# Cross attention over eight batches: in the first batch, who normalises, who makes the low parts, and where the transposes are written

## The reference

```python
q = einsum('bcn,dc->bnd', x, Wq) + bq
k = einsum('bcn,dc->bdn', ctx, Wk) + bk[:, None]
v = einsum('bcn,dc->bdn', ctx, Wv) + bv[:, None]
attn = softmax(einsum('bnd,bdm->bnm', q, k), axis=2)
out = einsum('bcm,bnm->bcn', v, attn) + x
```

## Time and profile before

| | |
|---|---|
| median of 3 executions | 667.35 us (667.12 to 668.11) |
| the profiled execution's own time | 666.91 us |
| its span | 664.7 us |
| TensorE matmul busy | 650.7 us, 98% |
| VectorE, ScalarE, POOL busy | 461.1, 285.0, 138.2 us |
| granted TensorE clock over the span | 0.996 |

### The profile page before, as it was taken

How to read it: one execution, slowest core, us unless ns; L and a number is a source line. 1 busy time by engine, 2 the same in 40 slices (tenths; PEclk the granted TensorE clock), 3 DMA queues, 4 the chain that set the end, 5 groups by cost and what they waited for, 6 DMA issues and landing times.

```text
span 664.7 us, 8316 instructions
## 1 busy us (share of the span) xinstructions
PE 650.7 (98%) x2852; PEld 533.5 (80%) x2852; DVE 461.1 (69%) x506; ACT 285.0 (43%) x372; POOL 138.2 (21%) x57
## 2 busy tenths in 40 slices
PE   8978899999999999999999999999999999999998
PEld 5766788888888888888888888888888888888886
DVE  5956768696586785786767867769668696586541
ACT  6656523456235362354433743337432456135120
POOL 0266300053002430033200430006300063002100
PEclk9999899999999999999999999999999999999999
DMA  8900732874428733496325863167621875325352
GB/s 314 329 6 1 175 96 78 223 239 125 126 77 233 232 96 121 114 308 160 101 88 139 306 167 101 64 158 269 172 95 63 200 265 135 121 71 139 72 158 88
DMA packets 94253, 100.09 MB, mean 151 GB/s; under 512 B 7328, under 2 KB 69024, under 8 KB 94240
## 3 DMA queue, kind: packets, MB, share of 16 engines
q1 hardware_dynamic: 94240, 99.91, 50.5%
HBM read 51.64 MB, written 16.78 MB: 103 GB/s over the span
## 4 chain that ended last, share of the span: by engine, by line
PE 90%; DVE 3%; POOL 1%; DMA 1%; issue 1%; ACT 1%; SPq 1%; DVEq 0%; POOLq 0%
PE acc_ps L854 51%; PE acc_ps L823 23%; PE s_ps L793 8%; PE s_ps L801 4%; PE s_ps L802 4%; DMA stage<-in_x_dram 1%; DVE pt_lo L532 1%; POOL blocks L299 1%; DVE negmax L592 1%; POOL probs L299 1%; DVE k_ll L532 0%; PE acc_ps L924 0%; ACT pt_hi L326 0%; SPq L256 0%; DVE vt_lo L532 0%
## 5 line engine op out<-in xcount | busy, mean ns | idle before, releaser
L854 PE MATMUL acc_ps<-pt_hi,vt_hi 128*128 128x512 f32 x512 | 199.4, 390 | 0.6 <-issue 0.6
L854 PE MATMUL acc_ps<-pt_hi,vt_lo 128*128 128x512 f32 x512 | 199.3, 389 | 0.0
L854 PE MATMUL acc_ps<-pt_lo,vt_hi 128*128 128x512 f32 x512 | 199.3, 389 | 0.0
L390 ACT ACTIVATE probs<-s_ps,negmax 128x1024 f32<-128x1024 f32 x60 | 67.0, 1117 | 122.4 <-DVE negmax L592 122.4
L285 POOL TENSOR_TENSOR pt_lo<-pt_raw,pt_hi 128x1024 fp32r<-128x1024 f32 x14 | 41.0, 2950 | 356.9 <-ACT pt_hi L326 356.9
L854 PEld LDWEIGHTS acc_ps<-pt_hi,vt_hi 128*128 128x128 f32 x512 | 96.2, 188 | 21.2 <-issue 1.0
L854 PEld LDWEIGHTS acc_ps<-pt_lo,vt_hi 128*128 128x128 f32 x512 | 96.2, 188 | 20.1
L854 PEld LDWEIGHTS acc_ps<-pt_hi,vt_lo 128*128 128x128 f32 x512 | 96.1, 188 | 20.0
L285 POOL TENSOR_TENSOR xs_lo<-stage,xs_hi 128x1024 fp32r<-128x1024 f32 x28 | 74.0, 2645 | 86.0 <-ACT xs_hi L326 86.0
L823 PE MATMUL acc_ps<-wv_hi,xs_hi 128*128 128x512 f32 x224 | 87.1, 389 | 0.0
L823 PE MATMUL acc_ps<-wv_lo,xs_hi 128*128 128x512 f32 x224 | 87.1, 389 | 0.0
(11 more groups left out here) (82 smaller groups left out, 673.7 us busy)
## 6 DMA issues: line engine op xcount, KB each, us to landing
pt_raw<-blocks SPq DMA_DIRECT2D x240, 128.0 KB, 2.4
stage<-in_x_dram SPq DMA_DIRECT2D x32, 512.0 KB, 6.2
o_sb<-in_x_dram SPq DMA_DIRECT2D x64, 256.0 KB, 3.3
out_dram<-o_sb SPq DMA_DIRECT2D x64, 256.0 KB, 2.4
stage<-in_ctx_dram SPq DMA_DIRECT2D x31, 512.0 KB, 8.8
pt_raw<-in_L_xattn_Wv_dram SPq DMA_DIRECT2D x4, 256.0 KB, 6.5
stage<-in_ctx_dram SPq DMA_DIRECT2D x2, 256.0 KB, 3.7
pt_raw<-in_L_xattn_Wk_dram SPq DMA_DIRECT2D x1, 128.0 KB, 3.0
```

Of the source, the lines that this page charges most:

```text
L390: nc.scalar.activation(probs[:, t % 2, :], s_ps[:, t % 2, :, :].rearrange("p a n -> p (a n)"), ACT.Exp, bias=negmax[:, t:t + 1], accum_out ...
L854: mm = nc.tensor.matmul(acc_ps[:, c % BANKS, :], v[:, m, cols], p[:, m, :], start=(m == 0 and v is vt_hi and p is pt_hi), stop=(m == MT - ...
```

## The change

In the first batch only. POOL keeps the low part of Wq, and of batch 1 takes the low parts of x for k = 0, 1, 2 in place of 0, 2. VectorE takes all four low parts of x of batch 0; it normalises tiles 0 to 3, and ScalarE normalises tiles 4 to 7. The upper half of `k_ll` is copied by ScalarE from the lower. The transposes of tiles 0 and 1 go to banks 2 and 3 of `acc_ps`, those of tile 2 to the first and those of tile 3 to the second pair of `s_ps`. On TensorE scores 5 come behind the first output tile, scores 6 one tile earlier, value group 4 starts one q step later, and group 7 is split in two, around the turns. VectorE's list for batch 0 is written out instead of being the loop's first pass.

```diff
 def t_banks(t):
+    return acc_ps[:, 2:4, :] if t < 2 else s_ps[:, t % 2, :, :]
 # POOL
-for k in (0, 2): x0_lo of k
-first_normalise(probs0[:, t, :], t)  for t in 0..3;  first_normalise(probs[:, t % 2, :], t)  for t in (4, 5)
+for k in range(KT - 1):
+    x1_lo(1, k)
+rest(1)
+with pool.Fori(2, B) as b:
+    x1_lo(b, 0)
+    x1_lo(b, 2)
+    rest(b)
 # ScalarE
+def first_k_high(half):
+    act.wait_ge(s_ksum, 1)
+    copy(k_hh[half * D:(half + 1) * D, :], full[:]).then_inc(s_khi, 1)
+def first_k_lo_copy():
+    act.wait_ge(s_klo, 1)
+    copy(k_ll[D:2 * D, :], k_ll[0:D, :].bitcast(F32)).then_inc(s_klo, 1)
 first_x1_hi(1)
+first_x1_hi(2)
 first_k_cross()
-first_x1_hi(2)
 first_v_hi(0)
 first_x1_hi(3)
+first_k_high(0)
 first_v_hi(1)
-k_high(0)
+first_k_high(1)
+first_v_hi(2)
 first_q_cross()
-first_v_hi(2)
 first_q_high_a()
+first_k_lo_copy()
+first_q_high_b()
 first_v_hi(3)
-first_q_high_b()
 first_v_hi(4)
...
 first_p_hi(1)
-first_v_hi(7)
 first_p_hi(2)
 first_p_hi(3)
+first_v_hi(7)
+round_x1(1, 0)
+round_x1(1, 1)
 exp(0, 4)
 exp(0, 5)
+first_normalise(4)
+exp(0, 6)
+first_normalise(5)
+exp(0, 7)
+first_normalise(6)
+first_normalise(7)
 # in batch(0, first=True), before round_x1(1, 2), round_x1(1, 3):
-round_x1(nb, 0); round_x1(nb, 1); exp(b, 6); first_normalise(6); exp(b, 7); first_normalise(7)
 # VectorE
+def first_normalise(t):
+    inverse(t)
+    dve.wait_ge(s_inv, t + 1)
+    nc.vector.tensor_scalar(probs0[:, t, :], probs0[:, t, :], inv[:, t:t + 1], None,
+                            ALU.mult).then_inc(s_norm, 1)
-first_x1_lo(1)
+for k in range(KT - 1):
+    first_x1_lo(k)
 first_k_sum()
 first_v_lo(0)
 first_x1_lo(3)
 first_v_lo(1)
-k_low(0)
+first_k_low()          # lower half only
 first_q_sum()          # waits s_khi 2 and s_klo 1 in place of s_klo 2
+first_q_low_a()
 first_v_lo(2)
-first_q_low_a()
 first_v_lo(3)
-first_v_lo(4)
 neg_max(0, 0)
 neg_max(0, 1)
-first_q_low_b()
-inverse(0)
-inverse(1)
+first_v_lo(4)
+first_normalise(0)
+first_normalise(1)
+neg_max(0, 2)
 first_v_lo(5)
-neg_max(0, 2)
 neg_max(0, 3)
 first_p_lo(0)
-inverse(2)
+first_normalise(2)
+first_normalise(3)
 first_v_lo(6)
-inverse(3)
 first_p_lo(1)
-first_v_lo(7)
+first_q_low_b()
 first_p_lo(2)
 first_p_lo(3)
+first_v_lo(7)
 neg_max(0, 4)
 neg_max(0, 5)
 inverse(4)
+neg_max(0, 6)
 inverse(5)
 turn(0, 4, first=True)
-neg_max(0, 6)
+neg_max(0, 7)
 turn(0, 5)
-neg_max(0, 7)
 inverse(6)
+inverse(7)
 turn(0, 6)
-inverse(7)
+batch(0, False, first=True)   # low_x1(1, 1) replaced by a wait for POOL's
 # TensorE
-first_q(0); first_q(1); first_v_group(4, part=0); first_q(2); first_q(3)
+first_q(0); first_q(1); first_q(2); first_v_group(4, part=0); first_q(3)
...
 first_v_group(6, part=1)
+first_v_group(7, part=0)
 first_turn(1)              # waits for the low part of tile 0
-first_v_group(7)
 first_turn(2)              # waits for no low part
 first_turn(3)
+first_v_group(7, part=1)
 pe.wait_ge(s_qlo, 1)
-scores_next(0, 4)
-scores_next(0, 5)
 pe.wait_ge(s_plo, 2)
+scores(4)
 # in batch(0): scores(5) at (c, m) = (0, 1); scores_next(0, 6) at (0, 5) in place of (0, 6)
```

More of the change, by code:

```diff
@@ L60 @@
 V_BANK0 = (0, 1, 2, 3, 0, 1, 0, 1)
-T_BANK0 = (2, 2, 2, 0)
 def build(nc, x1_d, x2_d, wq_d, bq_d, wk_d, bk_d, wv_d, bv_d, out_d):
@@ L178, in build, with t_banks @@
         block = ctx.enter_context(nc.Block())
+        def t_banks(t):
+            return acc_ps[:, 2:4, :] if t < 2 else s_ps[:, t % 2, :, :]
         def turned(t):
-            return acc_ps[:, T_BANK0[t]:T_BANK0[t] + 2, :].rearrange("p a (m r) -> p (a m) r", r=Q)
+            return t_banks(t).rearrange("p a (m r) -> p (a m) r", r=Q)
         def pt_tile(pt, t):
@@ L292, in _ @@
             low(wq_s[:, :, D:2 * D], wq_raw, wq_s[:, :, 0:D]).then_inc(s_wqlo, 1)
[L293 to L304, removed]
             def p_lo(b, j):
@@ L310, in p_lo, with x1_lo, rest @@
                     pt_hi[:, 2 * j:2 * j + 2, :]).then_inc(s_plo_odd, 1)
[L312 to L315, removed]
+            def x1_lo(b, k):
+                pool.wait_ge(s_x1hi, b * KT + k + 1)
+                low(xs_lo[:, k, :], stage1[:, k, :], xs_hi[:, k, :]).then_inc((s_x1lo_e, s_x1lo_o)[k % 2], 1)
+            def rest(b):
                 for i, k in enumerate((0, 2)):
-                    pool.wait_ge(s_x2hi, b * KT + KT + i + 1)
+                    pool.wait_ge(s_x2hi, b * KT + i + 1)
                     low(xs_lo[:, k, :], stage2[:, k, :], xs_hi[:, k, :]).then_inc(s_x2lo_e, 1)
-                p_lo(b + 1, 1)
-                p_lo(b + 1, 3)
+                p_lo(b, 1)
+                p_lo(b, 3)
+            for k in range(KT - 1):
[5 more added lines that the diff above has]
+                rest(b)
         @block.scalar
@@ L430, in batch @@
                 if first:
-                    round_x1(nb, 0)
-                    round_x1(nb, 1)
-                    exp(b, 6)
                     round_x1(nb, 2)
-                    first_normalise(6)
-                    exp(b, 7)
                     round_x1(nb, 3)
-                    first_normalise(7)
                 else:
@@ L545, in first_q_sum @@
                 dve.wait_ge(s_bqv, 2 * 16)
-                dve.wait_ge(s_klo, 2)
+                dve.wait_ge(s_khi, 2)
+                dve.wait_ge(s_klo, 1)
                 dve.wait_ge(s_qcross_a, 1)
@@ L562, in first_q_low_b, with first_k_low @@
                 sub(q_st[D:2 * D, NH:N], full[:, NH:N], q_st[0:D, NH:N]).then_inc(s_qlo, 1)
+            def first_k_low():
+                dve.wait_ge(s_khi, 1)
+                sub(k_ll[0:D, :], full[:], k_hh[0:D, :]).then_inc(s_klo, 1)
             def first_k_sum():
@@ L657, in v_phase, with batch @@
                 normalise(b, 7)
-            def batch(b, last):
+            def batch(b, last, first=False):
                 nb = b + 1
@@ L664, in batch @@
                 if not last:
-                    low_x1(nb, 1)
+                    if first:
+                        dve.wait_ge(s_x1lo_o, 3)
+                    else:
+                        low_x1(nb, 1)
                     low_x1(nb, 3)
@@ L725, in first_x1_lo @@
                 dve.wait_ge(s_x1hi, k + 1)
-                sub(x0_lo[:, k, :], stage1[:, k, :], x0_hi[:, k, :]).then_inc(s_x1lo_o, 1)
+                sub(x0_lo[:, k, :], stage1[:, k, :], x0_hi[:, k, :]).then_inc((s_x1lo_e, s_x1lo_o)[k % 2], 1)
             nc.vector.memset(probs[:, 0, 0:NH], 0.0).then_inc(s_warm, 1)
@@ L769, in _ @@
             inverse(4)
+            neg_max(0, 6)
             inverse(5)
             turn(0, 4, first=True)
-            neg_max(0, 6)
+            neg_max(0, 7)
             turn(0, 5)
-            neg_max(0, 7)
             inverse(6)
+            inverse(7)
             turn(0, 6)
-            inverse(7)
-            with dve.Fori(0, B - 1) as b:
+            batch(0, False, first=True)
+            with dve.Fori(1, B - 1) as b:
                 batch(b, False)
@@ L886, in batch @@
                     for m in range(MT):
-                        if first and (c, m) == (0, 6):
+                        if first and (c, m) == (0, 1):
+                            scores(5)
+                        if first and (c, m) == (0, 5):
                             scores_next(0, 6)
@@ L918, in first_turn @@
                     pe.wait_ge(s_acc, BANKS + 4)
[L919 to L922, removed]
+                elif t == 1:
+                    pe.wait_ge(s_plo, 1)
                 for m in range(MT):
-                    mm = nc.tensor.transpose(acc_ps[:, T_BANK0[t] + m // NT, (m % NT) * P:(m % NT + 1) * P],
+                    mm = nc.tensor.transpose(t_banks(t)[:, m // NT, (m % NT) * P:(m % NT + 1) * P],
                                              probs0[:, t, m * P:(m + 1) * P], ident[:])
@@ L1004, in _ @@
             first_q(1)
+            first_q(2)
             first_v_group(4, part=0)
-            first_q(2)
             first_q(3)
```

## The result

The changed kernel takes 662.83 us (median of 5, 662.09 to 664.0); the kernel before takes 667.21 (5 executions beside it). The ratio is 0.9935, 95% interval 0.992 to 0.9949: 4.3 us less. Two executions in the experiments, one of e2 (1391.45 us) and one of the kernel before beside e5 to e8 (937.07), fell in a slow state and are left out of the medians and ratios. The profiled execution took 662.09, its span is 660.2.

The account below looks back on a forecast made before the run. TensorE's waits in the first batch, their restarts and the clock dip were taken as the bound, about 10.8 us; 6.0 won by the projection, less 0.3 for handovers, gave 5.7: 661.65 from 667.35, range 660.6 to 665.2.

Parts of the forecast that it names:

- The path up to the projection: First batch up to batch 1's q projection: the projection ends at 66.6 against 72.59, 6.0 us won.
- rival B: At the projection the clock falls again: 1.45 of the gain lost, 2.0 if the chain is later; 663.1 to 663.7, chance 0.23.
- the forecast's own range: Whole kernel: 660.8 to 662.4 us around the forecast of 661.65, chance 0.53.
- Up to the outputs: First batch: outputs start at 46.0 with scores 5 still to do, as good as 46.9 against 50.92; 4.0 us won.
- the first maximum: VectorE's first maximum, behind v_lo(3): at 30.25 in place of 30.81, keeping 0.55 of the 1.0 won.
- The projection: TensorE stops at 61.6 for x's low part k = 2, which POOL ends at 64.4; VectorE's k = 3 ends at 65.5.
- The clock: Behind the projection's wait of 2.6 us the granted clock was taken to hold; if not, the gain is 1.45 less.
- 0.2 of slack: Second half's 16 moves: read at 75.0, rounding and low part done at 77.3, TensorE asking at 77.5.
- Rival C: VectorE or the moves take over the wait, at scores(4) or the second half's first tile: 663.5 to 664.6, chance 0.14.
- The lists for tiles 4 to 7: Chain of maxima, exponentials, ScalarE scalings and turns before the projection: turn 7 ends at 62.3, before 67.15.
- the 1.0 won at the first scores: First scores start at 28.65 in place of 29.61, with the key's low part copied on ScalarE in 1.07 us.

Follow-up runs that it names:

- e2: Changed kernel with tiles 4 to 7 normalised by VectorE in place of ScalarE, each turned right after, in a changed order: 659.49 us, ratio 0.9886.
- e5: Changed kernel with tiles 0 to 3 normalised by POOL again, VectorE making only their reciprocals: 667.56 us, ratio 0.9997.
- e8: Changed kernel with tiles 4 to 7 normalised by VectorE and both key low halves subtracted on VectorE: 658.72 us, ratio 0.9867.
- e6: Changed kernel with the old banks for the transposes of tiles 0 to 3, their waits and value group 7's old place: 664.55 us, ratio 0.9957.
- e3: Changed kernel with both low halves of the key subtracted on VectorE, no copy on ScalarE: 661.8 us, ratio 0.9911.
- e1: Changed kernel with 13 unread matmuls more on TensorE, filling its wait for x's low part k = 2 of batch 1: 661.56 us, ratio 0.9917.
- e4: Changed kernel with x's low parts k = 0, 2 of batch 0 on POOL again: 662.68 us, ratio 0.9935.
- e7: Changed kernel with ScalarE rounding x k = 2 of batch 1 ahead of scaling 7 in place of behind it: 662.68 us, ratio 0.9928.
- e9: e8 with the low half of q's second half moved on VectorE to ahead of the fourth maximum: 658.92 us, ratio 0.987.
- e10: e9 with tile 7 scaled by ScalarE and batch 1's x low part k = 2 on VectorE in place of POOL: 659.4 us, ratio 0.9878.
- e12: e9 with POOL's low part k = 1 of batch 1 held back until tile 5 is normalised: 658.84 us, ratio 0.9865.
- e11: e9 with tile 4 alone scaled by ScalarE, between exponentials 4 and 5: 657.6 us, ratio 0.9852.

## Why the prediction was right, and where it was off

The forecast was 661.7 in a range of 660.6 to 665.2; it measured 662.83. The path up to the projection was right, the clock there was not, and the range held the result because it took in rival B. The result lies outside the forecast's own range, 660.8 to 662.4.

*Up to the outputs.* Right in mechanism and nearly in size: POOL's waits went, VectorE works without a gap from 37.49 to 47.0, and the outputs start at 46.55 for 46.0. e5 and e6 show that both causes are the stated ones. Of the half microsecond, 0.3 is the first maximum (30.57 for 30.25): v_lo(3) on VectorE waits for v_hi(3), which stands on ScalarE behind the key's copy and q's second high part and came later than I had it.

*The projection.* The wait of 2.65 and its cause, the low part k = 2, were right, as was VectorE's part behind POOL's (63.51 + 2.46 = 65.97, with POOL's end at 64.88: 1.09). TensorE went on at 64.94 for 64.45.

*The clock* is the step that was off: "The new one is 64.45 - 61.85 = 2.6. I take 'holds'". It fell, at the price of rival B (1.45 in the text; 1.5 between the two groups of e3), and what came is B, 0.3 below its 663.1 to 663.7. e1, with the wait filled, keeps the clock up and ends the projection 1.1 earlier. What failed was to read a limit between 1.24 and 3.49 into a single execution. I count a dip where the granted clock over the whole execution is 0.997 or less (3.4 us at half the clock are 0.003 of the span). It came in 5 of 5 executions of the changed kernel, 5 of 5 of e4, 11 of 11 of e5, 4 of 5 of e6 and 3 of 5 of e3, together 28 of 31, all with waits of 2.63 or 2.65 in their profiles; in one of 5 with the 1.62 of e7; in none of the 12 of e9, e10 and e12, with waits of 0.49 to 1.09 at the projection. In the kernel before, with 3.49, it came in 36 of the 37 executions beside the experiments, and the one without it took 665.78. A wait gives a chance of the dip, not a yes or no.

*Behind it.* The moves fit as computed: they begin at 63.31 and are read at 75.87, 12.56 behind. The prediction gave them 0.2 of slack with the clock up; e1, e2 and e7 show that it is used up at once: TensorE then waits 0.19, 1.01 and 1.80 at the second half's first tile, and e7 keeps 0.5 of the 1.9 that it wins at the projection (its end at 66.69, less 0.23, against 68.34). Rival C named this place; its times are a slip, since a gain of 3.2 to 4 off 667.35 is 663.35 to 664.15 and not 663.5 to 664.6.

*Not seen* was that two parts of the change work against it. The lists for tiles 4 to 7 were followed right, but not compared with another engine or order, and cost some 3 us against e2. The key's copy was booked with the 1.0 won at the first scores, but VectorE was idle ahead of q's sum (24.6 to 26.2 by the prediction's own times, 2.05 us in the trace), and without the copy the first scores have no wait at all (e3).

## What to carry to other kernels

Where a tile passes from engine to engine, follow the handovers and the order of both lists as well as the busy time, and look for a place where both engines stand idle (here 2.33 and 2.65 us) while work for them is ready. Which engine should then do the scaling is no general rule: of the lists run here the fastest has tile 4 on ScalarE and the others on VectorE. Before moving work off an engine, look whether that engine idles ahead of the very step. And when a wait goes, name the next release behind it (here 16 moves, 12.6 us from release to reading) before booking the gain, since it caps what the earlier step can give.

## What the runs showed of the hardware

VectorE's scaling of an SBUF tile by a column has one SBUF tensor as input and takes 0.75 us. It waited while POOL subtracted two SBUF tensors: it took 2.23 us in e9, 1.36 in e8 and 3.00 in e12, each time ending 0.54 or 0.55 us behind POOL's operation. It goes the other way too: POOL's subtraction took 2.95 us in place of 2.40 where VectorE's scaling went first (e11). VectorE's maxima over PSUM and its transposes ran beside POOL at their own pace (1.22 and 1.25). No expectation before e11 counted POOL's two low parts at 45 to 50 us as in the way of a scaling. The Trainium skill ("SBUF — State Buffer", section "Who interferes with whom") states that `tensor_scalar` can contend with GpSimd for the shared ports, as operations with two SBUF inputs do; the prediction had used it only for the latter. It also states that the one issued first goes first; the traces agree except for e12, where VectorE's start is recorded 0.05 us earlier and it still waited.

TensorE's clock fell to the 1.2 GHz level behind waits of 2.63 or 2.65 us in 28 of 31 executions, and in one of five with a wait of 1.62 us (its place there was not profiled). With TensorE kept busy in that wait it did not fall in any of five (e1). An execution with the dip took 1.5 us more (e3). Granted clocks of 0.994 also occur, with 1 us more again (668.1 for 667.2 in the kernel before); where that second microsecond lies was not profiled.
